# Attention over a short context: the mask of the turned scores kept in two PSUM banks, one bank for the turned scores

## The reference, cut to what matters

```
q = (layernorm(x) @ Wq)                 # 8 batches, 128 tokens, 32 heads of 128
k, v = ctx @ Wk, ctx @ Wv               # 8 key heads, each shared by 4 query heads
q, k = rope(q), rope(k)
scores = q k^T / sqrt(128);  scores = where(mask == 0, -1e9, scores)
x = x + tanh(g0) * ((softmax(scores) @ v) @ Wo)
x = x + tanh(g1) * ffn(layernorm(x))    # silu gate of width 512, then a 512x512 product
```

## Time and profile before

| | |
|---|---|
| median of 3 runs | 736.09 us (735.6 to 737.16) |
| the profiled execution | 738.48 us, of which the span is 736.7 us |
| PE busy | 641.5 us, 87% of the span |
| DVE busy | 586.2 us, 80% |
| POOL busy | 451.6 us, 61% |
| ACT busy | 319.6 us, 43% |
| mean granted clock of TensorE | 0.981 of full speed |

### The profile page before, as it was taken

The page is one execution under the profiler, slowest core; times in us unless marked ns, Lnnn a source line. Parts: engine busy times, 40 slices in busy tenths (PEclk is TensorE's granted clock), DMA queues, the critical chain, the costliest instruction groups (busy, mean ns, idle before and its releaser), DMA issues.

```text
span 736.7 us, 10095 instructions
## 1 busy us (share of the span) xinstructions
PE 641.5 (87%) x2865; PEld 517.2 (70%) x2865; DVE 586.2 (80%) x1235; ACT 319.6 (43%) x892; POOL 451.6 (61%) x374
## 2 busy tenths in 40 slices
PE   8999999868888877888888887778888789999998
PEld 7888887756666666666666666666666668888886
DVE  3987658879989999899889989988998389887433
ACT  4347325444444444444444444444444246764320
POOL 6359669767777766676677667666777356630200
PEclk9999999989999999999999999999999989999999
DMA  9988952366464656565555555565534240400002
GB/s 309 315 261 277 332 192 76 125 194 198 151 209 148 215 171 187 170 201 170 173 176 182 186 167 180 186 187 181 193 122 150 65 129 20 113 0 1 1 15 100
DMA packets 133990, 118.38 MB, mean 161 GB/s; under 512 B 9776, under 2 KB 104496, under 8 KB 133936
## 3 DMA queue, kind: packets, MB, share of 16 engines
q1 hardware_dynamic: 132512, 116.69, 49.8%
q0 software_dynamic: 384, 1.05, 0.4%
q10 hardware_dynamic: 1040, 0.00, 0.1%
HBM read 72.89 MB, written 44.83 MB: 160 GB/s over the span
## 4 chain that ended last, share of the span: by engine, by line
PE 81%; issue 12%; DVE 2%; DMA 2%; ACT 1%; POOL 1%; SPq 1%; DVEq 0%; ACTq 0%; POOLq 0%
PE f_bank L644 10%; PE o_bank L644 10%; PE f_bank L646 10%; PE f_bank L645 10%; PE o_bank L646 9%; PE o_bank L645 9%; PE pv_bank L644 3%; PE pv_bank L645 3%; PE pv_bank L646 3%; PE s_banks L644 3%; PE s_banks L646 2%; PE s_banks L645 2%; PE s_banks L777 1%; PE t_bank L646 1%; PE t_bank L644 1%
## 5 line engine op out<-in xcount | busy, mean ns | idle before, releaser
L644 PE MATMUL o_bank<-wo_hi,o_hi 128*128 128x512 f32 x248 | 104.1, 420 | 80.0 <-issue 80.0
L1064 ACT ACTIVATE prob<-prob,small 128x128 f32<-128x128 f32 x256 | 99.7, 391 | 155.8 <-DVE small L1625 145.4
L1355 POOL TENSOR_TENSOR prob<-prob,small 128x512 f32<-128x512 f32 x64 | 66.7, 1042 | 139.4 <-DVE small L1656 139.3
L1625 DVE CUSTOM_DVE_ANT_0 prob<-s,mfill 128x128 f32<-128x128 f32 x192 | 142.7, 795 | 2.3 <-DMA s<-s_scratch 2.3
L644 PEld LDWEIGHTS o_bank<-wo_hi,o_hi 128*128 128x128 f32 x248 | 48.4, 195 | 107.6 <-issue 98.9
L644 PE MATMUL f_bank<-xT_hi,wq_hi 128*128 128x512 f32 x256 | 100.9, 394 | 0.3 <-DVE t_sin L1528 0.3
L646 PE MATMUL o_bank<-wo_hi,o_lo 128*128 128x512 f32 x248 | 100.2, 404 | 0.0
L646 PE MATMUL f_bank<-xT_hi,wq_lo 128*128 128x512 f32 x256 | 100.1, 391 | 0.0
L645 PE MATMUL f_bank<-xT_lo,wq_hi 128*128 128x512 f32 x256 | 100.1, 391 | 0.0
L645 PE MATMUL o_bank<-wo_lo,o_hi 128*128 128x512 f32 x248 | 99.9, 403 | 0.0
L1528 DVE TENSOR_TENSOR t_sin<-f_bank,rope 64x512 f32<-64x512 f32 x128 | 88.2, 689 | 2.7
(11 more groups left out here) (183 smaller groups left out, 1419.5 us busy)
## 6 DMA issues: line engine op xcount, KB each, us to landing
p_scratch<-p_blk SPq DMA_DIRECT2D x51, 256.0 KB, 2.0
p<-p_scratch SPq DMA_DIRECT2D x51, 256.0 KB, 2.9
s_scratch<-s_blk SPq DMA_DIRECT2D x48, 256.0 KB, 2.1
s<-s_scratch SPq DMA_DIRECT2D x48, 256.0 KB, 2.9
k_scratch<-ks_parts SPq DMA_DIRECT2D x16, 512.0 KB, 3.1
raw<-in_L_xattn_Wq_dram SPq DMA_DIRECT2D x32, 256.0 KB, 3.7
raw<-in_L_xattn_Wo_dram SPq DMA_DIRECT2D x32, 256.0 KB, 3.2
k_parts<-k_scratch SPq DMA_DIRECT2D x16, 512.0 KB, 5.1
```

The costliest lines, as they stand in the source:

```text
L644: nc.tensor.matmul(dst, st[0], mv_[0], start=start, stop=False)
L1064: e = nc.scalar.activation(prob[:, k, h, :], prob[:, k, h, :], ACT.Exp, bias=nmin[k][:, h:h + 1], scale=-1.0, accum_out=psum_row[k][:, h:h ...
L1355: nc.gpsimd.tensor_tensor(prob[:, k], prob[:, k], rrow[k].unsqueeze(2).to_broadcast([128, GH, S]), ALU.mult).then_inc(pool_norm, 1)
L1625: op = nc.vector.tensor_tensor_reduce(prob[:, k, h, :].rearrange("p (j a) -> p j a", j=4), scores[:, h], fill, 1.0, HUGE, ALU.add, ALU.min ...
```

## The change

`mfill2` goes. The rearranged mask lies in PSUM: batches 4 to 7 in the second half of `s_banks`, batches 0 to 3 in `t_bank`. `mask_columns` becomes two ACT copies of half the size, which wait until these banks are free. All turned scores go to the first half of `s_banks`, so that `scores(n)` waits for `score_blocks(n-1)` where it waited for `score_blocks(n-2)`. `mask_turned` takes the mask as its first input, from PSUM, and the scores as its second, from SBUF. The first unit behind the steps (n = 52), which uses all of `s_banks`, waits also until the last mask of that bank has been used, and unit 8, the first turned unit of batch 0, waits for the second copy.

```diff
--- before.py
+++ after.py
@@ -148,7 +148,6 @@
         p_blk = place("p_blk", [128, 2, GH * S], F32, at["k32"])
         s_blk = place("s_blk", [128, 2, GH * S], F32, at["cT_lo"])
         s32 = place("s32", [128, 2, GH * S], F32, at["cT_lo"] + 4096)
-        mfill2 = place("mfill2", [128, B, S], F32, at["cT_lo"] + 8192)
 
         def col(i, n=1):
             return small[:, i:i + n]
@@ -173,6 +172,7 @@
         s_parts = s_banks[:, :].rearrange("p (h two k) -> p h two k", h=GH, two=2)
         up_bank = [f_bank[0][:, :], f_bank[1][:, :], s_banks[:, 0:512], s_banks[:, 512:1024]]
         v_bank = [t_bank, pv_bank]
+        mask_bank = [t_bank[:, :], s_banks[:, 512:1024]]
 
         def sems(*names):
             return (sem(n) for n in names)
@@ -762,15 +762,16 @@
                 if k == 0:
                     pe.wait_ge(k_loaded[half], 16 * (2 * gg + c // 4 + 1))
                 if turned(n):
-                    if n < ST0 + 2:
+                    if n == ST0:
                         pe.wait_ge(dve_mask, ST0)
                     else:
-                        pe.wait_ge(dve_sblk, n - 1 - ST0)
-                    three(s_banks[:, 512 * k:512 * k + 512], (k_parts[:, half, b, 0:S], k_parts[:, half, b, S:2 * S]),
+                        pe.wait_ge(dve_sblk, n - ST0)
+                    three(s_banks[:, 0:512], (k_parts[:, half, b, 0:S], k_parts[:, half, b, S:2 * S]),
                           (q_hi[:, k].rearrange("p h s -> p (h s)"), q_lo[:, k].rearrange("p h s -> p (h s)")), True, True).then_inc(pe_score, 1)
                     return
                 if n == ST1:
                     pe.wait_ge(dve_sblk, ST1 - ST0)
+                    pe.wait_ge(dve_mask, ST1 - HB)
                 elif n >= 1:
                     pe.wait_ge(dve_mask, n)
                 for h in range(GH):
@@ -1133,13 +1134,14 @@
                 split_chunk(*pair_chunks(*u(n)[:2])[n % 2])
                 pT_hi_copy(*u(n - 1))
 
-            def mask_columns():
-
-                act.wait_ge(pe_v, 16)
-                act.wait_ge(pe_kq, ROT_ORDER.index(("K", KVH - 1, 1)) + 1)
-                act.wait_ge(dve_small, 4)
-                nc.scalar.activation(mfill2[:, :, :].rearrange("p b (j a) -> p b a j", j=4), mfill[:, :, :].rearrange("p b (a j) -> p b a j", j=4),
-                                     ACT.Copy).then_inc(act_mask2, 1)
+            def mask_columns(half):
+
+                if half:
+                    act.wait_ge(dve_mask, ST0)
+                else:
+                    act.wait_ge(dve_pTlo, HEAD_T)
+                hi(mask_bank[half].rearrange("p (b j a) -> p b j a", b=HB, j=4),
+                   mfill[:, HB * half:HB * half + HB, :].rearrange("p b (a j) -> p b j a", j=4), act_mask2)
 
             q_hi_copy(0, 1, 0)
             pT_hi_copy(0, 0, 0)
@@ -1153,7 +1155,8 @@
             exps(0, 1, 0)
             split_chunk(*pair_chunks(0, 1)[0])
             exps(0, 1, 1)
-            mask_columns()
+            mask_columns(1)
+            mask_columns(0)
             split_chunk(*pair_chunks(0, 1)[1])
             q_hi_copy(0, 2, 0)
             q_hi_copy(0, 2, 1)
@@ -1610,7 +1613,7 @@
                 if n >= ST0 + 2:
                     dve.wait_ge(s_stored[k], 16 * ((n - ST0) // 2))
                 nc.vector.transpose(s_blk[:, k, :].rearrange("p (i h a) -> p i h a", i=4, h=GH),
-                                    s_banks[:, 512 * k:512 * k + 512].rearrange("p (h i b) -> p i h b", h=GH, i=4)).then_inc(dve_sblk, 1)
+                                    s_banks[:, 0:512].rearrange("p (h i b) -> p i h b", h=GH, i=4)).then_inc(dve_sblk, 1)
 
             def mask_turned(gg, c, k):
 
@@ -1619,10 +1622,12 @@
                 prob_free(n)
                 if n == ST0:
                     dve.wait_ge(act_mask2, 1)
+                elif n == ST0 + HB:
+                    dve.wait_ge(act_mask2, 2)
                 scores = s32[:, k, :].rearrange("p (j h a) -> p h j a", j=4, h=GH)
-                fill = mfill2[:, n % B, :].rearrange("p (j a) -> p j a", j=4)
+                fill = mask_bank[n % B // HB].rearrange("p (b j a) -> p b j a", b=HB, j=4)[:, n % HB]
                 for h in range(GH):
-                    op = nc.vector.tensor_tensor_reduce(prob[:, k, h, :].rearrange("p (j a) -> p j a", j=4), scores[:, h], fill, 1.0, HUGE,
+                    op = nc.vector.tensor_tensor_reduce(prob[:, k, h, :].rearrange("p (j a) -> p j a", j=4), fill, scores[:, h], 1.0, HUGE,
                                                         ALU.add, ALU.min, nmin[k][:, h:h + 1])
                 op.then_inc(dve_mask, 1)
```

## The result

The changed kernel takes 666.56 us (median of 4 runs, 663.93 to 668.68), the kernel before 736.62 in the same session (4 runs, 735.6 to 737.29). The ratio is 0.9048, interval 0.9007 to 0.9089: 9.5% faster. The forecast was 656 with a range of 643 to 686, so the sign and the range held, and the saving was 70 us where 80 were forecast. But 666.56 lies above the 647 to 664 that the forecast held for likeliest (0.55), in the stretch from 664 to 690 that it gave to rival 1 (0.25).

A forecast was written before the change was run, and what follows sets the result against it. PE waits each step for out_proj behind DVE's masking, which POOL blocks. Steps from 8.72 to 7.05 us (6.83 + 0.12 + 0.1) save 76.8, the head 3.5: 738.5 becomes 658.2, as a median 656 us; range 643 to 686.

The forecast's parts named there:

- rival 1: In the steps, the probabilities' store and load through DRAM become the bound: 7.4 us a step, 672 us; chance 0.25.
- Rival 2: The masking on DVE still waits for POOL despite a single SBUF input; only the copy gains, 736 us; chance 0.05.
- The PSUM price: Masking input from PSUM: by the skill's rule 65 ns longer each, up to 4.6 us in all; left out of the sum.
- Rival 3: DVE comes late to score_blocks and the one bank stops PE at scores: 741 us at 8.9 a step; chance 0.05.
- The floor: PE's 30 matmuls a step without waits, taken as 6.83 us against 8.72.
- rival 4: No price for v loads and no thin margins in the steps: 6.83 us a step, 644 us; chance 0.10.
- 1 us in eight steps, 0.12 a step: Charge for the two v loads that stand in front of the probabilities' store in one step of eight.
- the 2.47 us from store to load: Time from the probabilities' store to their load, used in the two-step loop of 13.3 us, 6.67 a step.
- thin margins: Charge of 0.1 us a step, for slack of only 0.2 and 0.3 us in the steps.
- The loop through DRAM: Two-step chain from norm through the probabilities' store and load to POOL: 13.3 us, 6.67 a step, 0.2 below PE.
- The average share leaves room: Argument against DRAM transfers becoming the bound, with the DMA share forecast to rise from 0.56 to about 0.7.
- the signs named beforehand: For a wrong price: PE waits over 1 us once in eight steps, or each step before pv or scores, POOL awaiting pT_hi.

The follow-up runs named there:

- the reordered kernel: Changed kernel with the loads of k and v issued right behind the probabilities' load instead of ahead of their store: 652.49 us, ratio 0.8858.

## Why the prediction was right, and where its sum was off

**The cause was right.** The masking waited for POOL because both inputs were in SBUF. In one kernel the moved masks lost the wait and the others kept it, the swapped inputs changed nothing, and the medians of 285 and 286 ns over 192 instructions agree with the 286 of L1646 in the earlier trace rows. Rival 2 is out. The Trainium skill has this as a rule: the page "SBUF — State Buffer", section "Who interferes with whom", says that a DVE instruction with two SBUF inputs contends with a GpSimd instruction that reads SBUF, and that one with at most one SBUF input, outside the modes that use both ports, does not. The rows agree: 785 ns against 278 in one execution.

**The PSUM price was rightly left out.** The four maskings follow each other by 0.21 us, as two unblocked ones did in the earlier trace rows, and the median of 285 to 286 ns stands 7 ns above the shortest with both inputs in SBUF. The 65 ns more, worked out as an estimate from the Trainium skill's page "VectorE: DVE Perf Modes", section "The TRN2 errata — SBUF-src ops pay a fixed extra latency per instruction", are not in these rows.

**One bank cost nothing in the steps,** as forecast, and 0.6 us at the entry, where at most 0.7 was. Rival 3 is out: DVE is 265.74 us busy in 334.99, and the bank is waited for at one place.

**The floor was right:** 6.83 a step was taken, 6.82 came where the k and v loads were cut away (6.80 in the single step). The working beside it, 30 times 3.40/15, makes 6.80; with that the step would have been 7.02 and the forecast 1.4 us lower. That kernel, at 641.84 us, is what rival 4 described: its step is there to be had only without these loads in the way.

**The term that was mis-sized is the loads.** The sum charged "1 us in eight steps, 0.12 a step", for v alone. The runs put the loads of k and v at 0.47 a step, 3.7 us in eight. Two steps of the working led there. The loads of k have no term in it, and no reason is given for that. Before, they went out 3.9 to 4.5 us ahead of the next store, which then landed after 2.0 to 2.9 us. These rows of the timeline of before show one.

```profile
354.57 0.49 SPq L456 DMA_DIRECT2D k_parts<-k_scratch  x1
...
359.09 0.33 SPq L512 DMA_DIRECT2D p_scratch<-p_blk  x1
...
362.43 0.32 SPq L536 DMA_DIRECT2D s_scratch<-s_blk  x1
...
362.86 0.37 SPq L522 DMA_DIRECT2D p<-p_scratch  x1
```

The store landed after 2.0 us here; that the load comes only 3.77 us behind it is due to the store of the scores at 362.43, which stands between them on SP. With the change DVE comes to `p_blocks` earlier, and the k load goes out later, since the load of the probabilities that stands ahead of it on SP waits itself (235.39 above). In six of the eleven k loads in the steps the distance fell to 0.57 to 1.35 us, and there the store took 5.0 to 6.5 us to land. And the 2.47 us from store to load were taken from rows of a longer step, as if they were a property of the transfer, though the landing depends on what went out just ahead. The other 0.1 a step, for thin margins, was not needed: without the loads nothing of it is left.

**Rival 1 came true in part.** The loop through DRAM does bind, in about half of the steps, and 7.28 lies nearer to that rival's 7.4 than to the 7.05 of the forecast. That the stated range held is due to the room that it left for this rival. Its numbers fit in part: the DMA share is 0.69 (0.7 said), the store's median landing rose from 2.0 to 3.1 us, but the load's stayed at 2.9. Its reason, fuller engines, is not what the runs show for most of it: the reordered kernel has the same share and 15.9 us less of the 21.4. "The average share leaves room", the argument against it, was beside the point for these, since their delay comes from one transfer standing next to another. Of the signs named beforehand, the wait of POOL for `pT_hi` appeared, but PE stopped in front of `out_proj` and not `pv` or `scores`.

**The sum, mended.** In the profiled execution: 658.2 forecast, +10.7 in the steps (334.99 less 46 times 7.05), -1.6 at the entry, -3.3 in the tail, makes 664.0, and 663.93 was measured. The median of the runs lies 2.6 above that execution. At the entry the wait of 5.14 us became 1.21 as the first masking shrank from 4.13 to 0.85 us; the mask copies gained nothing, 1.08 and 1.06 us for what took 2.10. The tail is most likely not the change's doing: it is also 173.2 us with one bank and the mask in SBUF, and 172.4 in the kernel before with its loads moved. What made it 176.0 in the one execution of before is open.

## What to carry to other kernels

Where a DVE instruction with two SBUF inputs ends with a GpSimd instruction again and again, and one input is constant, put that input into a PSUM bank that can be spared: it took one copy of 1 us a bank and gave 9.5%. When a step becomes shorter, go through the transfers in program order and ask which of them now stand next to each other: a time from store to dependent load that was read in a longer step holds only for its neighbours there. Big loads that are not urgent did better here right behind the load that ends a round trip than ahead of the store that begins the next one.

## What was not expected of the hardware

In the changed kernel a store of the probabilities mostly lands right behind the transfer ahead of it, however late that one is. In the steps of before 29 of 46 stores of the probabilities landed after 2.0 to 2.1 us. In the changed kernel 6 of 47 did; 36 landed 0.5 to 0.8 us behind the transfer that SP had issued just ahead of them, whichever it was: 13 times a weight load, 12 times a load of v, 10 times a load of k and once a load of scores. So the 256 KB store with a 512 KB load of k 0.57 us ahead landed after 6.5 us, the load itself having taken 6.4. The bytes ahead make the difference and not the place in the queue alone: with a load of v 0.47 to 0.48 us ahead, the store of before took 3.1 to 3.5 us, and with that load cut to 32 columns 2.1. In the reordered kernel all 23 stores of this kind stand behind a weight load; no run moves those. The Trainium skill says in "DMA: Bandwidth & Descriptors", section "Two DMAs through the same engine are not ordered", that within one queue of a DMA engine descriptors start in order; the rows agree with a store that stands behind the load's data, though they don't show the queue itself.

An ACT copy of 512 scattered elements took 1.06 to 1.08 us into PSUM, half of the 2.10 us that 1024 took into SBUF. Since the scattered side is the input in the new copies and was the output in the old one, this does not show what the destination alone makes.

The time of the changed kernel also scatters more than that of the kernel before: 663.9 to 668.7 us in seven of the eight runs of its two groups (the eighth, 673.96, ran at a lower clock), against 735.4 to 737.9 for the eleven runs of before beside them. With the k and v loads cut away three of four runs lie within 1.1 us (641.25 to 642.32, one at 645.87). That the scatter comes from how the transfers fall beside each other is a guess from the 21 long steps; no run shows it alone.
